# One product of 128 rows for the bias of queries and keys, and one table of 39 expert tiles instead of two tables of 31 and 15

## The reference

```python
x = x + attn(_layernorm(x))           # 16 heads of 16, per sequence of 64
x = x + xattn(_layernorm(x), ctx)     # 16 heads, keys and values from a 64-wide context
x = x + ffn(_layernorm(x))

# attn:  q = (layernorm(x, g, b) @ Wq + bq), kv = (layernorm(x, g, b) @ Wkv + bkv), rotary, layernorm of each head, softmax
# ffn, 8 experts of 256 hidden units, each row goes to its best 2:
probs = softmax(x @ Wr); topk_w, topk_idx = top_k(probs, 2); topk_w = topk_w / sum(topk_w)
for i in range(8):
    w_i = sum(topk_w * (topk_idx == i))
    output = output + w_i * (silu(x @ Wg[i]) * (x @ Wu[i])) @ Wd[i]
```

## Time and profile before

| | |
|---|---|
| runs | 681.92 us median (681.84 to 682.16) |
| profiled execution | 682.53 us, its span 680.3 us |
| granted TensorE clock, mean | 0.973 |
| PE, DVE, ACT, POOL busy | 92%, 74%, 51%, 38% |
| self-attention / cross-attention / experts | about 0 to 210 / 210 to 541 / 541 to 680 us |

### The profile page before, as it was taken

How to read it: one execution, slowest core, us unless ns; L and a number is a source line. 1 busy time by engine, 2 the same in 40 slices (tenths; PEclk the granted TensorE clock), 3 DMA queues, 4 the chain that set the end, 5 groups by cost and what they waited for, 6 DMA issues and landing times.

```text
span 680.3 us, 15361 instructions
## 1 busy us (share of the span) xinstructions
PE 624.4 (92%) x5650; PEld 467.5 (69%) x5650; DVE 504.0 (74%) x1210; ACT 348.3 (51%) x1206; POOL 257.5 (38%) x233
## 2 busy tenths in 40 slices
PE   3787999998899999999999999999978899999991
PEld 2556777777788567676676666776745688888881
DVE  4898899998467797648986499855887965745585
ACT  1467999998581015721267022750448656455540
POOL 2104000000003855733376643866427233464331
PEclk9897999998799999999999999999989999999997
DMA  8799990000000000000000300002063133343467
GB/s 286 180 368 326 339 313 8 2 2 2 1 1 17 16 1 3 1 16 1 2 2 9 105 13 2 1 18 94 2 204 124 55 86 88 107 135 125 137 197 240
DMA packets 42008, 61.77 MB, mean 91 GB/s; under 512 B 15280, under 2 KB 36272, under 8 KB 41328
## 3 DMA queue, kind: packets, MB, share of 16 engines
q1 hardware_dynamic: 36528, 49.23, 23.8%
q0 software_dynamic: 3744, 10.26, 4.1%
q10 hardware_dynamic: 1664, 1.31, 0.7%
HBM read 48.44 MB, written 31.38 MB: 117 GB/s over the span
## 4 chain that ended last, share of the span: by engine, by line
PE 73%; DVE 9%; ACT 8%; issue 3%; DMA 3%; POOL 2%; SPq 1%; another core or an unknown queue 0%; POOLq 0%; ACTq 0%; DVEq 0%
PE bank L361 62%; PE bank L370 11%; DMA wkv_s<-in_L_xattn_w_kc_kv 2%; DVE m L1146 2%; ACT kbd L1570 1%; DVE wlo L1427 1%; ACT vbd L1556 1%; POOL r L1838 1%; ACT ex L1690 1%; SPq L1906 1%; ACT ex L1580 1%; ACT xth L1536 1%; DMA gb<-results 1%; DVE x L1493 0%; DMA results<-ys,place 0%
## 5 line engine op out<-in xcount | busy, mean ns | idle before, releaser
L1838 POOL TENSOR_TENSOR r<-m,m 128x512 f32<-128x512 f32 x80 | 104.4, 1329 | 101.2 <-DVE m L1146 87.6
L1146 DVE TENSOR_TENSOR m<-bank,cst 128x512 f32<-128x512 f32 x192 | 121.9, 685 | 24.0 <-PE bank L361 18.9
L1690 ACT ACTIVATE ex<-bank,nmax 128x64 f32<-128x64 f32 x256 | 73.1, 340 | 27.5 <-DVE nmax L1393 27.5
L361 PE MATMUL bank<-xth,wbh 128*128 128x512 f32 x192 | 80.1, 417 | 0.1
L361 PE MATMUL bank<-xth,wbl 128*128 128x512 f32 x192 | 75.3, 392 | 0.0
L361 PE MATMUL bank<-xtl,wbh 128*128 128x512 f32 x192 | 75.0, 391 | 0.0
L1673 ACT ACTIVATE qc<-bank 128x512 f32<-128x512 f32 x32 | 17.4, 595 | 100.0 <-PE bank L361 100.0
L1886 POOL DMA_INDIRECT results<-ys,place x46 | 44.4, 965 | 63.1 <-ACT ys L1765 55.3
L361 PE MATMUL bank<-wop,qc 128*128 128x256 f32 x256 | 62.5, 389 | 0.3 <-DVE x L1422 0.2
L361 PEld LDWEIGHTS bank<-wop,qc 128*128 128x128 f32 x256 | 46.4, 189 | 15.6 <-issue 9.2
L1580 ACT ACTIVATE ex<-bank,nmax 128x64 f32<-128x64 f32 x256 | 54.2, 360 | 1.6 <-DVE nmax L1048 1.5
(11 more groups left out here) (221 smaller groups left out, 1505.0 us busy)
## 6 DMA issues: line engine op xcount, KB each, us to landing
slots<-in_fill SPq DMA_DIRECT2D x1, 13416.0 KB, 52.5
xs<-slots SPq DMA_DIRECT2D x46, 129.0 KB
slots<-in_fill SPq DMA_DIRECT2D x1, 5160.0 KB, 61.0
gb<-results SPq DMA_DIRECT2D x16, 256.0 KB
wo_s<-in_L_xattn_Wo SPq DMA_DIRECT2D x1, 2048.0 KB, 17.4
wq_s<-in_L_xattn_Wq SPq DMA_DIRECT2D x1, 2048.0 KB, 11.7
wraw<-in_L_ffn_Wg SPq DMA_DIRECT2D x8, 256.0 KB, 3.7
wraw<-in_L_ffn_Wu SPq DMA_DIRECT2D x8, 256.0 KB, 3.9
```

What stands on the lines that cost most here:

```text
L361: return e.matmul(o, l, r, start=start, stop=stop, skip_group_check=True)
L1146: last = e.tensor_tensor(m4[n % 2][m][:, :].rearrange("p (b s) -> p b s", s=S), products[half][:, :].rearrange("p (b s) -> p b s", s=S), t ...
L1690: last = e.activation(ex[b % 4][:, h * 64:(h + 1) * 64], score_banks(b)[odd][:, n * 64:(n + 1) * 64], ACT.Exp, bias=nmax[b % 4][:, 4 * odd ...
L1838: last = e.tensor_tensor(rope[n % 6][half][:, :], m4[n % 2][first][:, :], m4[n % 2][second][:, :], op)
```

## The change

1. The bias: DVE writes a tile `crows` of 128 rows whose row 0 is the high part of the bias, row 1 the low part and all others zero; one product of 128 rows (ones against crows) replaces the two of one row. The tile of ones is filled earlier.
2. One list and one numbering for all rows (capacity 2048 for each expert). A first table holds 17 tiles that are surely full after three blocks (WHOLE); a second holds the 22 others: for each expert what is left of the first three blocks, then what block 3 adds. In all 39 tiles instead of 46. The fill of `slots` is one transfer of 17408 rows instead of two of 13312 and 5120.
3. The last routing stands in steps -1 to 8 instead of 0 to 16, its scatters two to a step behind stores 5 to 8 of GpSimd's list, and the combines of row tiles 0 to 11 in steps 36 to 40 (2, 2, 2, 3, 3), since 31 tiles must be stored before the first.

```diff
-PARTS_OF = ((0, 3), (3, 4))
-CAP = [4 * P * (hi - lo) for lo, hi in PARTS_OF]
-TILES = [2 * c // P + E - 1 for c in CAP]
+EARLY = 3
+CAP = NT * P
+WHOLE = -(-(2 * 4 * P * EARLY - E * (P - 1)) // P)
+TILES = [WHOLE, 2 * NT + E - 1 - WHOLE]
+EARLY_DONE = (2 * 4 * P * EARLY + E * (P - 1)) // P
...
-        ROUTE_LAST = {"stats": 0, "norm": 2, "T": 4, "logits": 6, "max": 6, "exp": 8, "rank": 9, "pos": 13, "slots": 14}
-        COMBINE_AT = TILES[0] + 7
+        ROUTE_LAST = {"stats": -1, "norm": 0, "T": 1, "logits": 2, "max": 2, "exp": 3, "rank": 4, "pos": 6, "slots": 6}
+        LAST_SCATTERS = {5: (0, 1), 6: (2, 3), 7: (4, 5), 8: (6, 7)}
+        COMBINES = {EARLY_DONE + n: c for n, c in ((5, (0, 1)), (6, (2, 3)), (7, (4, 5)), (8, (6, 7, 8)), (9, (9, 10, 11)))}
...
-                mm(e, o[:, :], onesr[0:1, :], crh[0:1, :], False, False)
-                mm(e, o[:, :], onesr[0:1, :], crl[0:1, :], False, True).then_inc(s_qk, 1)
+                mm(e, o[:, :], onesr[:, :], crows[:, :], False, True).then_inc(s_qk, 1)
...
-                e.tensor_copy(crh[:, :], crow[:, 0:512]).then_inc(s_crh, 1)
+                e.tensor_copy(crh[:, :], crow[:, 0:512])
+                e.tensor_scalar(crl[:, :], crow[:, 0:512], C("biasrow")[:, 0:1], None, ALU.mult).then_inc(s_crh, 1)
                 w.wait_ge(s_crh, 1)
-                e.tensor_tensor(crl[:, :], crow[:, 0:512], crh[:, :].bitcast(F32), ALU.subtract)
-                e.tensor_copy(onesr[:, :], C("ones")).then_inc(s_csplit, 1)
+                e.scalar_tensor_tensor(crows[:, :], crh[:, :].bitcast(F32), C("biasrow")[:, 1:2], crl[:, :], ALU.mult, ALU.add).then_inc(s_csplit, 1)
...
+            def late_ends():
+                w.wait_ge(r_route, RK * 4)
+                w.wait_ge(r_tab, TAB)
+                e.tensor_reduce(early[:, :], full[:, :, :], AX, ALU.add).then_inc(r_tab, 1)
...
+                e.tensor_tensor(spans[:, E:2 * E], stops[:, E:2 * E], starts[:, E:2 * E], ALU.subtract)
+                e.tensor_tensor(gap[:, :], starts[:, 1:2 * E + 1], stops[:, :], ALU.subtract).then_inc(r_tab, 1)
...
-            route_step(3, 0, ROUTE_LAST)
+            route_step(3, -1, ROUTE_LAST)
             for i in range(sum(TILES)):
-                t, half = divmod(i - ROUTE_LAST["slots"], 3)
-                if 0 <= t < 4 and half < 2:
+                for n in LAST_SCATTERS.get(i, ()):
                     w.wait_ge(t_hT, i + 2)
-                    scatter(3, 2 * t + half)
+                    scatter(3, n)
                 store(i)
...
-                if 0 <= i - COMBINE_AT + 3 < 12:
-                    results_load(i - COMBINE_AT + 3)
-                if i == COMBINE_AT + 6:
-                    result(0, 4)
+            for t in range(8):
+                results_load(t)
+            result(0, 4)
+            for t in range(8, 12):
+                results_load(t)
             result(4, 8)
             result(8, 12)
```

More of the change, by code:

```diff
@@ L71, in constants @@
     c["tri"] = (p[:, None] < p[None, :]).astype(np.float64)
[L72 to L75, removed]
+    c["ebase"] = np.tile(i[None, :] * CAP, (P, 1))
+    n = np.arange(2 * E)
+    c["le"] = np.tile((n[None, :] <= n[:, None]).astype(np.float64).reshape(1, -1), (P, 1))
+    c["next"] = np.tile(np.where(n == E - 1, 1 - E, n < 2 * E - 1)[None, :], (P, 1))
+    c["fill"] = np.tile(P * np.arange(TILES[1])[None, :], (P, 1))
+    c["iota"] = np.tile(np.arange(TILES[1])[None, :], (P, 1))
     c["part"] = p[:, None]
@@ L242, in decoder @@
         mxhat = s4("mxhat", [P, 4, D + 2])
+        tables = Space(nc, s4.at)
         mxT = s4("mxT", [P, KD, 512])
[L244 to L250, removed]
+        past, pastgap = tables("past", [P, TILES[1], 2 * E]), tables("pastgap", [P, TILES[1], 2 * E])
+        upto = tables("upto", [P, 2 * E, 2 * E])
+        assert tables.at <= s4.at
+        full = s4("full", [P, E, CAP // P])
+        whole = s4("whole", [P, E, EARLY * 4])
+        nwhole = s4("nwhole", [P, E])
+        taken = s4("taken", [P, E])
+        early = s4("early", [P, E])
+        used = s4("used", [P, E])
+        spans = s4("spans", [P, 2 * E])
+        ends = s4("ends", [P, 2 * E])
+        starts = s4("starts", [P, 2 * E + 1])
+        stops = s4("stops", [P, 2 * E])
+        gap = s4("gap", [P, 2 * E])
+        expert = s4("expert", [P, TILES[1]])
+        rowf = s4("rowf", [P, TILES[1]])
         eoff = s4("eoff", [P, COLS[1] + TILES[1]], I32)
@@ L1075, in weights @@
                 last.then_inc(s_bwide, 1)
+                e.tensor_copy(onesr[:, :], C("ones"))
                 w.wait_ge(d_w1, 32)
@@ new lines, in late_rows @@
+            def late_rows():
+                n, cols = TILES[1], slice(COLS[1], COLS[1] + TILES[1])
+                mine = slice(FIRST[1], FIRST[1] + n)
+                w.wait_ge(r_tab, TAB + 7)
+                e.tensor_scalar(own[:, mine], C("iota"), float(P), C("part"), ALU.mult, ALU.add)
+                e.tensor_tensor(pastnext[:, :, :], past[:, :, :], in_tiles(C("next"), n), ALU.mult)
+                e.tensor_tensor(pastgap[:, :, :], past[:, :, :], in_tiles(gap[:, :], n), ALU.mult).then_inc(r_tab, 1)
+                w.wait_ge(r_tab, TAB + 8)
+                e.tensor_reduce(expert[:, :], pastnext[:, :, :], AX, ALU.add)
+                e.tensor_reduce(rowf[:, :], pastgap[:, :, :], AX, ALU.add).then_inc(r_tab, 1)
+                w.wait_ge(r_tab, TAB + 9)
+                e.tensor_scalar(eoff[:, cols], expert[:, :], float(WE), None, ALU.mult)
+                e.scalar_tensor_tensor(own[:, mine], rowf[:, :], starts[:, 0:1], own[:, mine], ALU.add, ALU.add)
+                e.scalar_tensor_tensor(row[:, cols], rowf[:, :], starts[:, 0:1], C("fill"), ALU.add, ALU.add).then_inc(r_tab, 1)
+                w.wait_ge(r_tab, TAB + 10)
@@ L1918, in sync @@
             w.wait_ge(d_cst, 16)
-            for n, d in enumerate(slots):
-                rows = a["fill"][sum(ROWS[:n]):sum(ROWS[:n + 1]), :]
-                e.dma_start(d.rearrange("(p n r) d -> p n (r d)", p=P, r=4), rows.rearrange("(p n r) d -> p n (r d)", p=P, r=4)).then_inc(d_fill, 16)
+            e.dma_start(slots.rearrange("(p n r) d -> p n (r d)", p=P, r=4), a["fill"].rearrange("(p n r) d -> p n (r d)", p=P, r=4)).then_inc(d_fill, 16)
             w.wait_ge(s_S, 16)
@@ L2033 @@
     at["_"] = n
-    fill = np.zeros((sum(ROWS), D + 2), dtype=np.float32)
-    fill[:, D] = 2 * NT * P + np.arange(sum(ROWS))
+    fill = np.zeros((ROWS, D + 2), dtype=np.float32)
+    fill[:, D] = 2 * NT * P + np.arange(ROWS)
     fill[:, D + 1] = -1.0
```

134 lines of the change are left out of this document (78 added, 56 removed).

## The result

The changed kernel takes 674.12 us in the median of 4 runs (671.62 to 675.39), beside it the kernel before 682.04: ratio 0.9866, 95% interval 0.9846 to 0.9887. Predicted were 668.5 (663.5 to 675). The direction and the range held, the range with less than 1 us to spare; of the forecast gain of 13.4 us only 8.0 came.

What follows compares the result with a forecast made beforehand. TensorE was taken to bound the expert loop, no engine alone the middle of the self-attention. Terms -17.9 + 2.0 + 4.0 - 2.0 + 0.5 = -13.4 us, against the median 681.92, gave 668.5 us, range 663.5 to 675.

Steps and rivals of the forecast that it cites:

- three signs: Wrong if: loop period not 2.56 us, TensorE waits there above 5 us, self-attention ends over 4 us sooner or any later.
- Seven tiles, -17.9: Expert loop: 39 tiles instead of 46 save seven periods of 2.56 us, -17.9 us (bounds -17.5 to -18.2).
- The last routing, +2.0: First expert steps: the routing's bursts on DVE, in ten steps instead of seventeen, cost +2.0 us (bounds 0 to +5).
- I take 1.4 us of lag as free: Expert loop: DVE may run 1.4 us late in a tile; every microsecond beyond stalls TensorE.
- The end, +4.0: After the last tiles: combines that no longer hide beside tiles delay the last loads, +4.0 us (bounds +2.5 to +6).
- so they are just in time: End: loads of row tiles 4 to 11 take 2.84 us each, while four combines take 4.1.
- The bias, -2.0: Self-attention: TensorE saves 1.05 us per chunk, 0.39 comes through in five chunks, -2.0 us (bounds -8.4 to +1).
- Small edits, +0.5: First table's small operations +0.3 and wider constants +0.2, together +0.5 us (-0.5 to +1.5).
- C: Expert loop: tile 17's rows come too late for TensorE; 672, at most 677.5 us; chance 0.16.
- B: Self-attention: the bias gain comes through almost whole, 6.3 us instead of 2.0, giving 664.2 us; chance 0.12.
- D: Routing steps: waits for DVE bring TensorE's low clock, up to 692 us, slower than before; chance 0.04.
- E: Crowded DVE costs 5 us more in the loop and at the end than the summed forecast, 673.5 us; chance 0.12.

Runs made afterwards that it cites:

- combined: Also called the spread version: changed kernel with idle products, vectors first, ranks in three steps, table in four, loads_first's order of loads and writes; 665.98 us, ratio 0.9746.
- bias_alone: The kernel before with the one product of 128 rows for the bias and nothing else of the change; 678.92 us, ratio 0.9946.
- wide_constants: The kernel before with 203 unused columns at the end of the constants; 684.0 us, ratio 1.0017.
- late_writes: The changed kernel with SyncE's last list reordered, the write of rows 8 to 11 behind the loads of results 12 to 15; 672.54 us, ratio 0.9857.
- loads_first: The changed kernel with SyncE's last list as loads 0 to 7, write of rows 0 to 3, loads 8 to 15, then the other writes; 676.47 us, ratio 0.9886.
- after_again: The changed kernel itself, unchanged, run again as a control beside the others on their chip; 672.35 us, ratio 0.9838.
- table_in_four: The changed kernel with the second table's work on DVE spread over steps 7 to 10 instead of 7 and 8; 679.34 us, ratio 0.9913.

## Why the prediction was right, and where it was not

The number fell into the range because the largest term, the seven tiles, was right; the last routing, the end and the start came out worse, some 5.4 us together, and the range had room for that. Two of the three signs that the prediction named for being wrong were there: TensorE waits 5.6 us for DVE in the loop (more than 5), and the self-attention ends 0.86 us later (not sooner). The loop's period held.

**Seven tiles, -17.9:** right. The period is 2.54 us: -17.8.

**The last routing, +2.0:** it cost +3.1 (14.7 less instead of 17.8), inside the bounds. The step that failed is "I take 1.4 us of lag as free". The transposes of the next h wait for thl, not for gu: at 562.43 and 562.76 stand gu and thl, and TensorE goes on at 563.32, 0.15 behind thl's end (562.76 + 0.41). thl starts 0.34 behind gu and takes 0.41, so of the 1.91 us between gu and the transposes 1.16 are free. That alone doesn't make the difference: with 1.16 in place of 1.4 the prediction's own chain of lags would still have no stall in steps 4 and 6. It also let DVE enter step 4 in time. But round the exponentials ScalarE loads two tables of 1.28 us each, gu starts at 559.07 after a wait of 2.69 for ScalarE, and TensorE waits 0.72 behind it. The kernel before has these too (0.71 at 571.36); there the rank was in two steps, here its whole burst follows at once, and the next gu is late again. And the routing's own products, which wait for share, have no lag free at all (0.81). The waits for DVE in steps 4 to 8 are 0.62, 0.81, 0.67 and 1.21, 3.3 us where I had 1.2. The spread version, which in the loop changes only where DVE does this work and when the scatters follow, takes 2.7 us less. The bursts in the bound of this term add up to 9.8, not 10.1; nothing hangs on it. The kernel before had itself about 1.0 us of disturbance in its loop: `bias_alone` does its tiles 0 to 43 in 113.27 instead of 114.31, `wide_constants` in 113.21, so against a clean loop the routing cost +4.1.

**The end, +4.0:** +5.9. The computed chain of combines held (15.8 us without the wait), except for "so they are just in time". The loads of row tiles 8 to 11 stand beside the write of 512 KB and the last scatters, with the DMA engines' mean busy share at 0.97 from 652 to 657 us; the first of them lands after 5.1 us where I took 2.84: 1.71 us of wait. `late_writes` and `loads_first` show that the order of these transfers moves the waits, by up to 2 us.

**The bias, -2.0:** the net is near (-2.1 at the end of the self-attention in `bias_alone`), by luck: two errors cancel. "In the first three chunks ... I give them nothing" was wrong: the third chunk's last such product comes 1.4 us sooner (51.41, before 52.78), and 1.8 us were there at the first residual. By the fifth the gain is 3.58 (`bias_alone`); 0.45 in each chunk of the middle agrees with the 0.39 of the earlier trace rows. By the Trainium skill (TensorE: Matmul & The Clock Gate, Back-to-back issue gap) one product less in each of the six row tiles of the first three chunks would be an estimated 6 x 0.216 = 1.3; the 1.4 measured is close to it. Then the stretch at half clock began sooner and took 1.3 back; that was one bound of this term, and I had not put it into the value. After the sixth residual -2.26 is left.

**Small edits, +0.5:** the first table changed nothing that can be seen (543.80 - 200.05 = 343.75 from the seventh residual to the first tile, after 343.71). The constants were mis-sized: I scaled their own load by 13%, but the bias tiles wait for a vector queued behind them. 2.1 us late at the start in this execution. The changed kernel in `after_again`, started at 10.92, has its fifth residual at 150.70 instead of 153.32, so the late start cost 2.6.

**The rivals.** C, tile 17 too late: not in the changed kernel; TensorE doesn't wait for xs, and the eight scatters took 0.96 us each, beside the busiest steps of DVE; the slow-down that the Trainium skill (SBUF — State Buffer, Who interferes with whom) let me expect there does not show in this trace. It is a weak test of that rule, since the section names copies, casts and tensor_scalar, and steps 7 and 8 are mostly tensor_tensor and tensor_reduce. The slack was larger than my 2 us: tile 17's load is issued at 584.70 and lands after 3.5, 3.0 us before TensorE takes it at 591.16; one scatter turn later, and with a faster loop, `combined` waits 0.22. B: no, 0.45 came in a chunk and not 1.05. D: its mechanism exists (`loads_first` above: 2.00 us of wait, then 3 us at 0.50), also in the changed kernel (`after_again`, behind 0.80 us), but costs 1.5 to 2 us and not 24. My argument against it, that waits of around 1 us leave the clock at 1.00, holds in one of its two profiles. E named the size, 5 us more in the loop and at the end; measured 3.0 there, and 2.6 at the start.

**Open:** why GpSimd, and ScalarE in `table_in_four` (5.77 us ahead of one sg), stand still on two of the four chips near the scatters of the last routing. The profile names only an unknown queue. Why the clock falls behind the same wait in one execution and not in another is open too.

## What to carry to other kernels

Ask of every load that grows what is queued behind it, and who waits for that. When work moves from beside the tiles to the end, add up the bytes there as well as the engine's time. And where rows show TensorE at half clock behind a wait, the wait can cost several times its length: idle products in it are cheap, and worth trying first, with a look at the clock afterwards.

## What the hardware showed that I had not expected

- Twelve unread products of 128 columns in a wait of 1.82 us gave 5.3 to 6.5 us: granted clock 1.00 instead of 0.53 over 14 us, and both chunks behind it shorter.
- A small scatter beside large writes lands late: 5.6 us after its issue beside 1 MB, 4.7 to 5.8 beside 512 KB, 2.9 just ahead of them.
- The same instructions took 99.6, 101.1 and 104.2 us between tile 0 and tile 36 in three executions. The 1.5 us between the first two are a clock that fell behind a wait of 0.80 us in one of them; the third was on a chip where GpSimd stands still.
